# Turning round the experts' second product and moving the steps around it

## The reference, cut to what matters

```python
G, E, C, K = 2, 8, 160, 2            # groups of 4096 tokens, experts, capacity, choices
logits = x @ w_router;  probs = softmax(logits);  gate, idx = top_k(probs, K)
pos = cumsum(mask) * mask - 1         # a token's place in its expert; over 160: dropped
expert_in = tokens sent to (expert, place)          # E x G x 160 x 256
h = relu(expert_in @ wi)                            # wi: E x 256 x 1024
expert_out = h @ wo                                 # wo: E x 1024 x 256
y = sum over k of gate[k] * expert_out[slot k]
x = layernorm(x + y)
```

## Time and profile before

| | us |
|---|---|
| median of 3 runs | 4830.02 (4827.56 to 4838.83) |
| the profiled execution | 4828.89 |
| its span | 4827.1 |
| TensorE busy | 4518.8 |
| VectorE, ScalarE, GpSimd busy | 3535.6, 2783.8, 1025.5 |

### The profile page before, as it was taken

One profiled execution on the slowest core, in us unless ns is written; L12 is line 12 of the kernel. 1 busy time (PEld: TensorE's weight loads), 2 busy tenths in 40 slices (PEclk: granted clock), 3 DMA queues, 4 the chain that ended last, 5 costly groups with the idle time before them and its releaser, 6 DMA issues. The chain is left out here.

```text
span 4827.1 us, 65506 instructions
## 1 busy us (share of the span) xinstructions
PE 4518.8 (94%) x25453; PEld 1687.8 (35%) x25456; DVE 3535.6 (73%) x3881; ACT 2783.8 (58%) x5253; POOL 1025.5 (21%) x991
## 2 busy tenths in 40 slices
PE   8988888999997999999999999999999999999895
PEld 4434343666662222222222222222222232222374
DVE  2554446887787777898777888777888988898141
ACT  2222222333332777888777777777777767788511
POOL 2333325344431121000121110112111011000223
PEclk9999999999997999999999999999999999999998
DMA  3000100011211333212333222223222121122323
GB/s 101 29 20 23 57 9 19 9 46 46 83 49 56 110 102 101 63 47 70 101 101 116 66 77 73 83 96 127 63 81 80 52 71 60 70 72 74 105 93 58
DMA packets 233083, 333.24 MB, mean 69 GB/s; under 512 B 37026, under 2 KB 174308, under 8 KB 230724
## 3 DMA queue, kind: packets, MB, share of 16 engines
q1 hardware_dynamic: 229892, 321.19, 20.3%
q0 software_dynamic: 2880, 7.87, 0.9%
HBM read 221.50 MB, written 98.04 MB: 66 GB/s over the span
## 5 line engine op out<-in xcount | busy, mean ns | idle before, releaser
L1555 DVE TENSOR_REDUCE mx<-ps 128x1 f32<-128x1024 f32 x2048 | 2405.8, 1218 | 434.3 <-PE ps L717 431.7
L1307 ACT ACTIVATE Pb<-ps 128x512 f32<-128x512 f32 x4096 | 2201.7, 597 | 498.1 <-PE ps L717 493.8
L717 PE MATMUL ps<-QS,KS 98*128 98x512 bf16 x4096 | 1250.4, 386 | 16.7 <-ACT Pb L1307 5.4
L717 PE MATMUL ps<-Pb,VA 128*32 128x512 f32 x8192 | 1097.9, 608 | 0.1
L717 PE MATMUL ps<-KM,QM 64*128 64x512 bf16 x4096 | 661.0, 390 | 58.0 <-DVE mx L1555 55.9
L717 PEld LDWEIGHTS ps<-QS,KS 98*128 98x128 bf16 x4096 | 261.6, 98 | 1082.6 <-ACT Pb L1307 884.5
L717 PEld LDWEIGHTS ps<-KM,QM 64*128 64x128 bf16 x4096 | 179.4, 93 | 614.3 <-issue 347.8
L1877 POOL CAST mrow<-mres 16x128 bf16<-16x128 f32 x64 | 18.0, 280 | 1347.5 <-ACT mres L1137 1347.5
L717 PEld LDWEIGHTS ps<-Pb,VA 128*32 128x32 f32 x8192 | 161.4, 108 | 399.9 <-issue 398.9
L717 PE MATMUL ps<-wdT,hT 128*128 128x256 f32 (+1 forms) x768 | 195.3, 397 | 19.7 <-DVE X L1540 14.8
L1154 ACT ACTIVATE phi<-phi 128x1024 f32<-128x1024 f32 x64 | 67.6, 1057 | 223.6 <-DVE phi L1429 223.6
(11 more groups left out here) (250 smaller groups left out, 4517.8 us busy)
## 6 DMA issues: line engine op xcount, KB each, us to landing
QM<-qd SPq DMA_DIRECT2D x128, 256.0 KB
KM<-kd SPq DMA_DIRECT2D x128, 256.0 KB
qd<-parts SPq DMA_DIRECT2D x96, 256.0 KB, 2.8
kd<-parts SPq DMA_DIRECT2D x96, 256.0 KB, 2.8
QS<-qd SPq DMA_DIRECT2D x64, 384.0 KB
KS<-kd SPq DMA_DIRECT2D x64, 384.0 KB
vdr<-vst SPq DMA_DIRECT2D x64, 256.0 KB, 2.7
den<-rd SPq DMA_DIRECT2D x64, 256.0 KB
```

What stands on the lines that cost most here:

```text
L717: return eng.matmul(out, a, b, start=start, stop=stop, skip_group_check=skip)
L1307: eng.activation(Pb[(u - 1) % 9], o, ACT.Exp, bias=0.0, scale=0.25).then_inc(act_A, 1)
L1555: eng.tensor_reduce(mx4[qc % 2][:, 4 * i + q, h:h + 1], o, AX, ALU.max).then_inc(dve_D, 1)
```

## The change

Six edits that belong together.

- `ed`: wo is stationary (128 of its 256 output columns at a time), h moves (160 slots). 16 matmuls as before. The result is transposed, [128 x 2 x 160]; ScalarE copies it to a ring `yT` of four experts' columns.
- `yt`, new: for each block of 128 slots two transposes by TensorE into bank 5, a copy by ScalarE to one of six buffers `er`, a store by SyncE. `eu` has three banks for four.
- `yw` reads `er` directly, block by block, inside `experts_order`; `yo` and its buffers go.
- `experts_order` puts `yt` and `yw` of expert e-2 behind the first chunk of expert e.
- The outputs of chunks in n = 15 follow the tighter table `OUT_LAST`, and the finishing of tiles 48 to 63 has fewer empty places and its `fo` in pairs. `oa` of the last chunk stands ahead of what is left of the background.
- `second` and `final_order` are laid out anew: the routing of group 1 is bunched into a few places.

```diff
+OUT_LAST = {0: ("oa",), 2: ("ob", "oc"), 3: ("od",), 5: ("oe",), 6: ("og",)}
...
         yield [("fl", T0)]
-        for _ in range(3):
-            yield []
-        for j in range(4):
-            yield [("fo", T0 + j)]
+        yield from [[]] * (1 if T0 >= 48 else 3)
+
+        for j in range(0, 4, 2):
+            if T0 >= 48:
+                yield [("fo", T0 + j), ("fo", T0 + j + 1)]
+            else:
+                yield [("fo", T0 + j)]
+                yield [("fo", T0 + j + 1)]
...
 def experts_order(g):
-    yield [("xt", g, 0)]
-    yield [("xt", g, 1)]
+
+    came = lambda e: range((160 * e + 127) // 128, (160 * (e + 1) + 127) // 128)
+    done = lambda e: range(160 * e // 128, 160 * (e + 1) // 128)
+
+    def back(e):
+        yield from ([("yt", g, b), ("yw", g, b)] for b in done(e))
+
+    yield from ([("xt", g, b)] for b in came(0))
     for e in range(8):
-        for n in range(3):
-            yield [("eu", g, e, n)]
+        yield [("eu", g, e, 0)]
+        if e > 1:
+            yield from back(e - 2)
+        yield [("eu", g, e, 1)]
+        yield [("eu", g, e, 2)]
         if e < 7:
-            for b in range((160 * (e + 1) + 127) // 128, (160 * (e + 2) + 127) // 128):
-                yield [("xt", g, b)]
+            yield from ([("xt", g, b)] for b in came(e + 1))
         if e:
             yield [("ed", g, e - 1)]
+    yield from back(6)
     yield [("ed", g, 7)]
+    yield from back(7)
...
-    yield [("yo", g, 0), ("yo", g, 1)] if g else [("yo", g, 0)]
-    yield [("yw", g, 0), ("gp", g, 0)]
     if g == 0:
-        yield [("yp", g, 0)]
-        yield [("yo", g, 1), ("yn", g, 0), ("ys", g, 0)]
-        yield [("yw", g, 1), ("gp", g, 1)]
-        yield [("yp", g, 1)]
-        yield [("yn", g, 1), ("ys", g, 1)]
+        for f in range(2):
+            yield []
+            yield [("gp", g, f)]
+            yield []
+            yield [("yp", g, f)]
+            yield [("yn", g, f), ("ys", g, f)]
...
-                elif x % 16 in OUT and step > 16:
-                    for stage in OUT[x % 16]:
+                elif step > 16:
+                    for stage in (OUT_LAST if m == 15 else OUT).get(x % 16, ()):
...
+    plan.extend([("oa", 15, 3)])
     while bg:
         background()
...
     def second():
-        for stages in (("oa",), ("ob", "oc"), ("od",), (), (), ("oe",), ("og",)):
+        for stages in (("ob", "oc"), ("od",), ("oe",), ("og",)):
             yield [(stage, 15, 3) for stage in stages]
...
-        yield []
-        for T in range(60, 64):
-            yield [("fo", T)]
-        yield [("we", 7), ("st2", 60), ("ap2", 60)]
-        ways = list(route_order(1))
-        yield sum(ways[:3], [])
...
+        yield from [[]] * 2
+        yield [("fo", 60), ("fo", 61)]
+        yield [("fo", 62), ("fo", 63)]
+        ways, inverse = list(route_order(1)), list(inverse_order(1))
+        yield [("we", 7), ("st2", 60), ("ap2", 60)] + sum(ways[:7], []) + [("of", 60)]
+        yield from [[]] * 6
+        yield sum(ways[7:], []) + inverse[0] + [("iv", 1, 1)]
+        yield from [[]] * 5
+        for j in range(8):
+            yield [("im", 1, j)] + ([("iv", 1, j + 2)] if j < 6 else [])
+        yield inverse[-1] + [("gx", 1, b) for b in range(10)]
...
-            for s in range(2):
+            for k in range(2):
                 for f in range(8):
-                    d = mm(bank(4)[0:80, 256 * s:256 * s + 256], h3[e % 2][:, f, 80 * s:80 * s + 80], wo[e][:, f, :], f == 0, f == 7)
+                    d = mm(bank(4)[:, 160 * k:160 * k + 160], wo[e][:, f, k * P:(k + 1) * P], h3[e % 2][:, f, :], f == 0, f == 7)
             d.then_inc(pe_ed, 1)
+
+        def yt(g, b):
+            x = 10 * g + b
+            w.wait_ge(act_ed, 8 * g + (P * b + P - 1) // 160 + 1)
+            w.wait_ge(act_yt, x)
+            c = P * (b % 5)
+            for k in range(2):
+                d = tr(bank(5)[:, P * k:P * k + P], yT[:, k, c:c + P])
+            d.then_inc(pe_yt, 1)
...
+        def yt(g, b):
+            x = 10 * g + b
+            w.wait_ge(pe_yt, x + 1)
+            if x > 5:
+                w.wait_ge(st_er[x % 6], 16 * (x // 6))
+                w.wait_ge(dve_mix, mix_at["yw", *divmod(x - 6, 10)])
+            copy(er[:, x % 6, :], bank(5)[:, 0:256]).then_inc(act_yt, 1)
```

More of the change, by code:

```diff
@@ L624, in program @@
     xr.append(take("xr0", [P, 10, 256]))
-    er = [take(f"er{i}", [P, 2, 256]) for i in range(2)]
-    assert top[0] <= mxr_at
+    er = take("er", [P, 6, 256])
+    assert top[0] <= mxr_at, (top[0], mxr_at)
     top[0] = low3
@@ L630, in program @@
     top[0] = hi3 + 1024
-    yown.append(take("yown0", [P, 5, 256]))
+    ypar.append(take("ypar0", [P, 5, 256]))
     assert top[0] <= route_at
     top[0] = mxr_at
-    ypar.append(take("ypar0", [P, 5, 256]))
+    yT = take("yT", [P, 2, 640])
     top[0] = 0
     ypar.append(take("ypar1", [P, 10, 256]))
-    top[0] = 8192
-    yown.append(take("yown1", [P, 10, 256]))
     half = lambda buf, g, f: buf[g][:, 5 * f:5 * f + 5, :] if g else buf[0]
@@ L683, in program @@
     ld_we = [sem(f"ld_we{i}") for i in range(8)]
-    ld_gx, st_of, st_fin, pool_of, dve_iv = (sem(n) for n in ("ld_gx", "st_of", "st_fin", "pool_of", "dve_iv"))
+    ld_gx, st_of, st_fin, pool_of, dve_iv, pe_yt, act_yt = (
+        sem(n) for n in ("ld_gx", "st_of", "st_fin", "pool_of", "dve_iv", "pe_yt", "act_yt"))
+    st_er = [sem(f"st_er{i}") for i in range(6)]
     a_of = lambda *step: a_no[step]
@@ L1106, in eu @@
             w.wait_ge(ld_we[e], 32)
-            if x > 4:
-                w.wait_ge(act_eu, x - 4)
-            o = bank((1, 2, 3, 5)[(x - 1) % 4])
+            if x > 3:
+                w.wait_ge(act_eu, x - 3)
+            o = bank(1 + (x - 1) % 3)
             c = 160 * e % 640
@@ L1716, in it, with yw @@
             eng.tensor_copy(tabs[g], tf).then_inc(dve_slots, 1)
-        def yw(g, f):
-            z, y = xr[g][:, 5 * f:5 * f + 5, :], half(yown, g, f)
-            w.wait_ge(pe_xt, 10 * (g + 1))
+        def yw(g, b):
+            z = xr[g][:, b, :]
+            w.wait_ge(pe_xt, at["xt", g, b])
             w.wait_ge(ld_gx, 160 * (g + 1))
[L1722 to L1726, removed]
+            w.wait_ge(act_yt, 10 * g + b + 1)
+            eng.scalar_tensor_tensor(out=z, in0=er[:, (10 * g + b) % 6, :], scalar=gt[g][:, 0, b:b + 1], in1=z,
+                                     op0=ALU.mult, op1=ALU.add).then_inc(dve_mix, 1)
         def yp(g, f):
             z, y = xr[g][:, 5 * f:5 * f + 5, :], half(ypar, g, f)
-            w.wait_ge(dve_mix, mix_at["yw", g, f])
+            w.wait_ge(dve_mix, mix_at["yw", g, 5 * f + 4])
             w.wait_ge(ld_gp[f], 80 * (g + 1))
@@ L1894, in gp @@
         def gp(g, f):
-            for k in range(2):
-                w.wait_ge(st_er[k], 64 * (g + 1))
+            for i in range(6):
+                w.wait_ge(st_er[i], 16 * ((10 * g + 15 - i) // 6))
             w.wait_ge(st_clear, 32)
@@ L1903, in gp @@
             else:
-                w.wait_ge(pe_V, 1024)
+                w.wait_ge(st_of, 256)
+                w.wait_ge(pe_D, d_of("fo", 63))
             y = half(ypar, g, f)
@@ L2119, in we, with yt @@
             load(flat(wo[e]), t["wo2"][e, :, :]).then_inc(ld_we[e], 16)
-        def ed(g, e):
-            i = e % 2
-            w.wait_ge(act_ed, at["ed", g, e])
-            load(eo[g][CAP * e:CAP * e + CAP, :].rearrange("(a p) d -> p a d", p=80), er[i][0:80]).then_inc(st_er[i], 16)
-        def yo(g, f):
-            for k in range(2):
-                w.wait_ge(st_er[k], 16 * (4 * g + 2 * f + 2))
-            if g:
-                w.wait_ge(pe_ed, 8 + 2)
-            elif f:
-                w.wait_ge(dve_mix, mix_at["yw", g, 0])
-            else:
-                w.wait_ge(st_of, 256)
-                w.wait_ge(pe_D, d_of("fo", 63))
-            load(half(yown, g, f), eo[g][640 * f:640 * f + 640, :].rearrange("(a p) d -> p a d", p=P)).then_inc(ld_own[f], 16)
+        def yt(g, b):
+            x = 10 * g + b
+            w.wait_ge(act_yt, x + 1)
+            load(eo[g][P * b:P * b + P, :], er[:, x % 6, :]).then_inc(st_er[x % 6], 16)
         stages = {"setup": setup, "rl": rl, "w0": w0, "wl": wl, "v": v, "fq": fq, "phase1": phase1, "ap1": ap1, "phase2": phase2,
                   "pl": pl, "ps": ps, "pv": pv, "fm": fm, "R2": R2, "fetch": fetch_group, "oa": oa, "oc": oc, "od": od, "og": og, "fl": fl, "ap2": ap2, "r0": r0, "of": of,
-                  "we": we, "ed": ed, "yo": yo}
+                  "we": we, "yt": yt}
         for step in plan:
```

32 lines of the change are left out of this document (12 added, 20 removed).

## The result

The changed kernel takes 4812.54 us (median of 5 runs, 4804.83 to 4819.92), the kernel before 4837.38 on the same chip: ratio 0.9953, interval 0.9942 to 0.9965. By the ratio that is 22.7 us faster where 41.0 were forecast; the two medians differ by 24.8, and this median of the kernel before is itself 7.4 above the 4830.02 that the forecast started from. The time lies above the range that I gave (4776 to 4806). The profiled execution was the slowest of its five: 4819.92, span 4818.1.

What follows compares the result with a forecast made beforehand. TensorE, busy 94% of the span, was taken to bound the kernel. Group 0 -26.9, group 1 -23.3, loop +8.0 and tail +1.2 summed to -41.0: span 4827.1 to 4786.1, forecast 4789 us, range 4776 to 4806.

Steps and rivals of the forecast that it cites:

- In the attention loop: Last attention chunks: moved out-projections 3.85, normalisation 1.3 and a TensorE idle of 2.8 make attention end 8.0 us later.
- the new waits of group 0: Experts' group 0: out-projection hand-overs 2.0, counting matmuls 2.4 and 1.0, first one-hot matmul 2.6 us.
- Second product: Experts' stage: turned round, it takes the first product's 4.35 us, saving 2.55 an expert, 20.4 for eight.
- transposes back: Experts' stage: twenty pairs of blocks at 0.22 us; with waits, 2.2 and 1.4 in group 0, 1.8 and 0.5 in group 1.
- tail: After the last product: more copies and transposes cost 1.7 us, faster gathers give 0.5 back; net 1.2 later.
- rivals 3 and 4: Experts' products: weight loads show, 4806, chance 0.03; block transposes stall TensorE, slower, 4873 if all twenty wait, chance 0.03.
- Tile 52's wait: In the loop, ahead of tile 52's out-projection, TensorE idles 2.8 us for the outputs of chunk (15,1).
- rival 1: New idles (2.8, 2.4, 2.6) in loop and group 0 lower the clock; one late ScalarE copy more: 4802, chance 0.17.
- (a): Group 0: TensorE's wait for the last attention chunk goes, its first transfer being issued earlier; 8.4 us gained.
- (b): Group 0: the idle of 4.10 at the routing's exp and the long product behind it go; 5.8 us gained.
- (c): Group 1: the idle of 4.23 for ScalarE's late copies goes with the own-result reload; 5.2 us gained.

Runs made afterwards that it cites:

- all three: Changed kernel with the first experts' weights issued later, group 1's routing later, and out-projections of tiles 52 to 55 two steps later; 4794.34 us, ratio 0.992.
- The product alone: Turned product, transposes back and new experts' order, but outputs, finishing and group 1's routing placed as in the kernel before; 4813.33 us, ratio 0.9978.
- the repeat: The changed kernel run once more, unaltered; 4816.36 us, ratio 0.996 to the kernel before.
- weights later: Changed kernel with the loads of three experts' weights (6 MB) issued five steps later, behind the output of chunk (14,3); 4813.11 us, ratio 0.9953.
- the first output by the old placing: Changed kernel with only the output of chunk (14,3) back on the old table; 4793.82 us, ratio 0.9941.
- the one-hot matmuls in pairs: Changed kernel with its eight one-hot matmul groups in pairs between first and second products, not between the transposes back; 4797.09 us, ratio 0.9949.
- the routing later: Changed kernel with group 1's first counting matmul and one-hot groups two entries later, second counting matmul behind the next second product; 4816.49 us, ratio 0.9961.

## Why the prediction was wrong

The direction and the product were right, the size was not. The step that failed is the account of what stands around the product, in two terms of the sum. "In the attention loop" was 8.0 and measured 17.4, because the output of chunk (14,3) was left out. And the new waits of group 0 were charged at their idle alone, with nothing for the rows at the lower clock: 107.65 forecast, 119.6 and 116.6 in the two traces of the changed kernel.

1. *Second product, transposes back, tail*: right. 4.35 each, 0.22 a block, tail 45.8 for 46.6; rivals 3 and 4 are refuted. A row of one-hot matmuls (x16: eight matmuls, each with two records and two loads) shows how near the loads were: 1.72 from its start to that of the next work (4612.45 to 4614.17 in all three with 50 columns, 4623.45 to 4625.17 with 128). So with 50 columns it isn't the moving side that sets the time, 107 ns a record; the load of 128 columns is the likely limit, though no run varied it alone. The product's 136 ns a record (4.35 by 32) lies above that.
   The Trainium skill, "TensorE: Matmul & The Clock Gate", section "LDWEIGHTS (loading the stationary operand)", counts a load's columns at 1.2 GHz, by which an estimate for 128 columns is 107 ns. The trace agrees at the full granted clock. At the lower one, which the rule doesn't treat, the same row takes 3.42 (4646.99 to 4650.41), 214 ns a record.
2. *In the attention loop: 8.0*. The first failed term. I worked through the outputs of (15,0) to (15,2) and never through that of (14,3), whose place the change moves too: 7.7, in all seven traces with its new place and the weights at step 0 (49.4 to 51.7), in none of the seven others (42.2). The rest of the loop, 8.0 forecast, measured 9.7, and that this is so near is partly luck: the trace of before has two idles of 1.45 and 2.17 just ahead of tile 52, with no releaser named. The product alone, with the same loop, took 172.0 from the mark of (14,3) to attention's end where before took 175.4; against it the rest of the loop costs 13.0. Tile 52's wait was seen in the right place; with its slow pair it was 5.8 instead of 2.8 (3.96 idle and 1.84), and two steps more of room take the segment from 50.5 to 44.5.
3. *New waits in group 0, and rival 1*. The second failed term: I charged idles and no clock. In the trace after, rows slower than their like at the full clock hold about 11.5, which is nearly all of the 12.0 over in group 0: 1.7, 1.7 and 1.3 in three products (4573.08, 4614.99, 4632.91), 6.0 in the rows from 4646.99 to 4659, 0.8 in two one-hot rows. Against this the waits were forecast 2.2 too high. This trace was the slowest of four with this layout of group 0: the others took 116.6 (the repeat), 113.85 (weights later) and 110.35 (the first output by the old placing). Rival 1, that the new idles lower the clock, is shown at tile 52 (1.84) and behind the counting matmuls (1.7). For the rest, 6.0 of it with no wait just ahead, the cause is open. As a number rival 1 came close: 9 for the clock and 4 for the late block gave 4802, and with the 7.7 of point 2 that is 4810 against a median of 4812.54. When the waits and the transfer were taken care of together, group 0 took 107.74 for 107.65 and the whole 0.992 for 0.9915. That this closes is partly luck. In group 0 the waits are 2.4 and not 6.0, and a first product ran 1.7 long; the loop was 4.4 shorter than forecast, and group 1 5.4 longer.
4. *(a) and (b)*: right. The transfer is issued at 4571.53, 0.9 us after attention's end, and neither the wait of 3.10 nor that of 4.10 is left. The product alone shows what they would have cost: 6.62 and 3.31.
5. *(c), "the least sure"*: wrong, and it cost 3.7 in group 1. Reloading the own results was not the cause of that wait. It is 2.54, with 6.19 for 4.51 behind it, after, 5.58 in the repeat, 4.19 in all three. Without the reload it is also absent in three traces with this order of group 1: the first output by the old placing, the product alone and the one-hot matmuls in pairs. ScalarE's records show it idle twice just then, with GpSimd's gathers in flight, and like pairs stand in the loop (the last segment 41.0 to 41.5 without, 44.3 to 48.1 with). The same gathers are in flight in the trace with the old placing, where there is no wait, so they alone don't explain it. Why ScalarE is late there is open.

Two things stay open: that cause, and what decides whether the clock comes back while TensorE is full. The idles of 1 to 2 us ahead of it go with the falls in some traces (1.60, then 0.50) and without in others (1.20 and 1.27, then 1.00). Nor was the segment of tile 52 tried alone; its share is read from the marks of all three, and by medians the 22.0 us are not divided among the three edits: each of the first two alone moved them by nothing measurable against the changed kernel on the same chip.

## What to carry to other kernels

When work is taken off a full engine, walk through every step whose place the edit moves, the first that it touches included, and look in the issuing queue for what stands ahead of each small transfer. Then ask of each chain beside the engine when it ends: the saving shows only where the engine was last (group 1, 21.8 us), and comes back as waits where the chain was (group 0, none). Price a new wait not at its idle alone but with the rows behind it at the lower clock: here 1.8 in the pair behind an idle of 3.96 at tile 52, and 1.7 in the product behind idles of 2.23 and 0.79 in group 0. Leave room beyond that, for the clock also fell in some executions with no such wait ahead.

## What the runs showed of the hardware

- With the routing later, TensorE's granted clock was 0.50 and then 0.57 in two stretches of 10 us, in each of which it was busy 10.00; being busy did not by itself bring the clock back. The changed kernel and its repeat show 0.53 over one such stretch.
- Eight one-hot f32 matmuls, each with its own 128-column weights, take 1.72 us to the next work with 50 moving columns and with up to 128: in this row the added width cost nothing.
- An 8 KB transfer behind six of 1 MB in the same queue was 13.0 us from issue to use, and VectorE waited 5.19 for it. Ahead of them its data were used 7.7 after the issue (4368.62 to 4376.35) with no wait.
